# Attention softmax on eight cores: every second normalization on ScalarE, one merged copy out of PSUM

## The reference

```python
qkv = x @ Wqkv + bqkv
q, k, v = jnp.split(qkv, [D, D + KV], axis=-1)      # 16 heads of q, 4 of k and v, HD = 128
scores = jnp.einsum('bqhd,bkhd->bhqk', q, k) / HD
prob = jax.nn.softmax(scores, axis=-1)
out = jnp.einsum('bhqk,bkhd->bqhd', prob, v).reshape(b, s, D)
return out @ Wout + bout
# the layer: xn = layernorm(x); x + attention(xn) + experts(xn)
```

## Time and profile before

| | |
|---|---|
| median of 3 runs | 5502.65 us (lowest 5501.75) |
| the profiled execution | 5507.19 us, its span 5505.6 |
| spans of the cores | 5484.4 to 5505.6 us, core 6 the slowest |
| busy | PE 4952.2 (90%), DVE 1740.7 (32%), ACT 747.1 (14%), POOL 258.4 (5%) |
| chain that ended last | PE 86%, ACT 5%, DVE 4%, DMA 3%, issue 2% |
| attention | from 543 to 1134 us of the span |
| granted clock of the slowest core | mean 0.954 |

### The profile page before, as it was taken

The page is one execution under the profiler, slowest core; times in us unless marked ns, Lnnn a source line. Parts: engine busy times, 40 slices in busy tenths (PEclk is TensorE's granted clock), DMA queues, the critical chain, the costliest instruction groups (busy, mean ns, idle before and its releaser), DMA issues.

```text
span 5505.6 us, 63487 instructions; the slowest of 8 cores (5484.4 to 5505.6 us)
## 1 busy us (share of the span) xinstructions
PE 4952.2 (90%) x23551; PEld 2343.6 (43%) x24008; DVE 1740.7 (32%) x2608; ACT 747.1 (14%) x1045; POOL 258.4 (5%) x493
## 2 busy tenths in 40 slices
PE   3588666688999999999999999999999999999995
PEld 2434443343444444444444444444444444444443
DVE  3300666611232222323333322323223222333333
ACT  4311555521000000000000000000000000000000
POOL 0000000000000000000000000000000000000000
PEclk8589999999999999999999999999999999999997
DMA  5231000036444444444334444444444444434434
GB/s 171 77 63 30 1 1 1 1 58 104 73 73 74 75 74 73 74 74 75 70 70 78 73 73 77 74 75 75 73 73 73 74 75 74 73 69 71 79 54 122
DMA packets 79881, 378.32 MB, mean 69 GB/s; under 512 B 9696, under 2 KB 10848, under 8 KB 65248
## 3 DMA queue, kind: packets, MB, share of 16 engines
q0 software_dynamic: 70416, 323.03, 33.4%
q1 hardware_dynamic: 9168, 51.21, 2.9%
HBM read 688.80 MB, written 8.39 MB: 127 GB/s over the span
## 4 chain that ended last, share of the span: by engine, by line
PE 86%; ACT 5%; DVE 4%; DMA 3%; issue 2%; DVEq 0%; ACTq 0%; SPq 0%; POOLq 0%
PE ps_a L824 48%; PE ps_d L760 24%; PE ps_a L491 4%; ACT p_exp L578 3%; PE ps_a L682 2%; PE ps_a L563 2%; PE ps_c L792 1%; DMA x_re<-x_own 1%; PE ps_c L632 1%; PE ps_c L395 1%; PE ps_d L632 1%; DVE pnT L618 1%; DVE pn_sb L589 1%; DMA wgubuf<-gu 1%; PE ps_b L354 1%
## 5 line engine op out<-in xcount | busy, mean ns | idle before, releaser
L824 PE MATMUL ps_a<-xn_own,wgubuf 128*128 128x512 bf16 x12044 | 2692.1, 384 | 25.8 <-DMA wgubuf<-gu 11.9
L824 PEld LDWEIGHTS ps_a<-xn_own,wgubuf 128*128 128x128 bf16 x12288 | 1211.6, 99 | 1517.1 <-issue 103.3
L760 PE MATMUL ps_d<-hstash,wdbuf 128*128 128x512 bf16 x6016 | 1330.4, 379 | 10.8 <-DVE ffn_acc L770 0.4
L847 DVE TENSOR_TENSOR sg_sb<-ps_a,sg_sb 128x512 f32<-128x512 f32 x384 | 265.5, 691 | 2404.2 <-PE ps_a L824 2404.2
L760 PEld LDWEIGHTS ps_d<-hstash,wdbuf 128*128 128x128 bf16 x6144 | 595.9, 97 | 741.3 <-issue 182.0
L770 DVE TENSOR_TENSOR ffn_acc<-ffn_acc,ps_d 128x512 f32<-128x512 f32 x1024 | 704.3, 688 | 605.6 <-PE ps_d L760 602.2
L837 ACT ACTIVATE sg_sb<-ps_a 128x512 f32<-128x512 f32 x384 | 229.2, 597 | 2261.1 <-PE ps_a L824 2261.1
L60 POOL DMA_DIRECT2D wgubuf<-gu x384 | 202.6, 528 | 2604.0 <-PE ps_a L824 2555.1
L563 PE MATMUL ps_a<-k_sb,q_sb 128*128 128x512 bf16 x470 | 136.1, 412 | 204.5 <-ACT p_exp L578 132.0
L852 DVE TENSOR_TENSOR hstash<-sg_sb,c_rep 128x512 bf16<-128x512 f32 x384 | 266.0, 693 | 42.7 <-DVE sg_sb L847 3.6
L802 ACT ACTIVATE c_rep<-ps_c 128x512 f32<-128x512 f32 x64 | 38.2, 597 | 1534.5 <-PE ps_c L792 1534.5
(11 more groups left out here) (104 smaller groups left out, 1408.2 us busy)
## 6 DMA issues: line engine op xcount, KB each, us to landing
wgubuf<-gu POOLq DMA_DIRECT2D x384, 512.0 KB, 5.2
wdbuf<-down POOLq DMA_DIRECT2D x64, 1536.0 KB, 10.9
xtile<-x_own SPq DMA_DIRECT2D x16, 1024.0 KB, 5.7
xtile<-x_nbr SPq DMA_DIRECT2D x16, 1024.0 KB, 5.5
wjbuf<-wqkv POOLq DMA_DIRECT2D x24, 512.0 KB, 5.1
woutbuf<-wout POOLq DMA_DIRECT2D x16, 512.0 KB, 5.2
x_re<-x_own SPq DMA_DIRECT2D x8, 1024.0 KB, 8.5
o<-out_sb SPq DMA_DIRECT2D x8, 1024.0 KB, 6.0
```

Of the source, the lines that this page charges most:

```text
L760: ins = e_.matmul(ps_d[:, slot * 512:(slot + 1) * 512], wdbuf[gh % 3][:, (dc % 8) * 768 + icc * 128: (dc % 8) * 768 + icc * 128 + 128], hs ...
L824: ins = e_.matmul(ps_a[:, bank * 512:(bank + 1) * 512], wgubuf[bufi][:, dc * 128:(dc + 1) * 128], xn_own[:, dc * TOWN + tb * 512: dc * TOW ...
L847: ev_h1[(e, ip, tb)] = B.op("vector", lambda e_, tb=tb: e_.tensor_tensor(sg_sb[:, tb * 512:(tb + 1) * 512], ps_a[:, (2 + tb) * 512:(3 + tb ...
```

## The change

In attention, the norm of odd i moves to ScalarE, as an Identity activation with the reciprocal as its scale; it is emitted at the end of `emit_softmax(i)`, after the wait for the reciprocal and, where there is one, for the transposes of i-2 that read the same pn buffer. Even i keeps it on VectorE. ps_b becomes 2,048 bf16 elements wide (two banks); the 16 transposes of one i fill it, and one VectorE copy of 2,048 replaces the two of 1,024. TensorE waits once, for the copy of the i before, ahead of all 16. ps_c is now a view of the second bank of ps_b, and PV writes the two halves of ps_d.

```diff
@@ -245,10 +245,9 @@
     nc.bump_sbuf(MBASE + 204800 - nc.sbuf_base)
 
     ps_a = nc.alloc_psum_tensor("ps_a", [128, 2048], F32).ap()
-    ps_b = nc.alloc_psum_tensor("ps_b", [128, 1024], BF16).ap()
-    ps_c = nc.alloc_psum_tensor("ps_c", [128, 512], F32).ap()
+    ps_b = nc.alloc_psum_tensor("ps_b", [128, 2048], BF16).ap()
     ps_d = nc.alloc_psum_tensor("ps_d", [128, 1024], F32).ap()
-    ps_b2 = ps_d[:, 512:1024].bitcast(BF16)
+    ps_c = ps_b[:, 1024:2048].bitcast(F32)
 
     B = Builder(nc)
 
@@ -360,7 +359,7 @@
             B.wait("vector", "st", ev_tpb[t][k])
             dst_view = xn_dst.rearrange("p (c q) -> p c q", c=DC)[
                 :, 8 * k:8 * k + 8, (t % 8) * 128:(t % 8) * 128 + 128]
-            src_view = ps_b.rearrange("p (c q) -> p c q", c=8)
+            src_view = ps_b[:, 0:1024].rearrange("p (c q) -> p c q", c=8)
             ev_tpb_evac[t][k] = B.op("vector", lambda e, d=dst_view, s=src_view:
                                      e.tensor_copy(d, s), "sv")
 
@@ -537,7 +536,7 @@
                 B.wait("vector", "st", evt)
                 dstv = vt_sb[:, (g * 16 + 8 * k) * 128:(g * 16 + 8 * k) * 128 + 1024]
                 ev_vt_evac_last = B.op("vector", lambda e, d=dstv:
-                                       e.tensor_copy(d, ps_b[:]), "sv")
+                                       e.tensor_copy(d, ps_b[:, 0:1024]), "sv")
 
     B.barrier()
 
@@ -571,7 +570,7 @@
         qb2 = i % 2
         B.wait("scalar", "st", ev_sc)
         if i >= 2:
-            B.wait("scalar", "sv", ev_normC[i - 2])
+            B.wait("scalar", ev_normC[i - 2][0], ev_normC[i - 2][1])
             B.wait("scalar", "sv", ev_biasC[i - 2])
         else:
             B.wait("scalar", "sv", ev_nz)
@@ -583,47 +582,52 @@
         B.wait("vector", "ss", ev_ln)
         ev_biasC[i] = B.op("vector", lambda e, qb2=qb2: e.tensor_tensor(
             nmax2[qb2][:], nmax2[qb2][:], lns2[qb2][:], ALU.subtract), "sv")
-        B.op("vector", lambda e, qb2=qb2: e.reciprocal(rssum[:], ssum2[qb2][:]))
-        if (i - 2, 1) in ev_tpC:
-            B.wait("vector", ev_tpC[(i - 2, 1)][0], ev_tpC[(i - 2, 1)][1])
-        ev_normC[i] = B.op("vector", lambda e, qb2=qb2: e.tensor_scalar_mul(
-            pn_sb[qb2][:], p_exp[qb2][:], rssum[:]), "sv")
+        ev_rc = B.op("vector", lambda e, qb2=qb2: e.reciprocal(rssum[:], ssum2[qb2][:]), "sv")
+        if i % 2 == 0:
+            if (i - 2, 1) in ev_tpC:
+                B.wait("vector", ev_tpC[(i - 2, 1)][0], ev_tpC[(i - 2, 1)][1])
+            ev_normC[i] = ("sv", B.op("vector", lambda e, qb2=qb2: e.tensor_scalar_mul(
+                pn_sb[qb2][:], p_exp[qb2][:], rssum[:]), "sv"))
+        else:
+            B.wait("scalar", "sv", ev_rc)
+            if (i - 2, 1) in ev_tpC:
+                B.wait("scalar", ev_tpC[(i - 2, 1)][0], ev_tpC[(i - 2, 1)][1])
+            ev_normC[i] = ("ss", B.op("scalar", lambda e, qb2=qb2: e.activation(
+                pn_sb[qb2][:], p_exp[qb2][:], AF.Identity, scale=rssum[:]), "ss"))
 
     def emit_tp(i):
         h, q = divmod(i, 8)
         qb2 = i % 2
-        B.wait("tensor", "sv", ev_normC[i])
+        B.wait("tensor", ev_normC[i][0], ev_normC[i][1])
+        if psb_gen[0] is not None:
+            B.wait("tensor", psb_gen[0][0], psb_gen[0][1])
         for k in range(2):
-            pbank = ps_b if k == 0 else ps_b2
-            if psb_gen[k] is not None:
-                B.wait("tensor", psb_gen[k][0], psb_gen[k][1])
-
-            def pt_batch(e, k=k, qb2=qb2, pbank=pbank):
+            def pt_batch(e, k=k, qb2=qb2):
                 for j in range(8):
                     kc = 8 * k + j
-                    ins = e.matmul(pbank[:, j * 128:(j + 1) * 128],
+                    ins = e.matmul(ps_b[:, k * 1024 + j * 128: k * 1024 + (j + 1) * 128],
                                    pn_sb[qb2][:, kc * 128:(kc + 1) * 128],
                                    ident_b[:], is_transpose=True,
                                    start=(j == 0), stop=(j == 7))
                 return ins
             ev_pt = B.op("tensor", pt_batch, "st")
             ev_tpC[(i, k)] = ("st", ev_pt)
-            dst_view = pnT.rearrange("p (c q2) -> p c q2", c=DC)[
-                :, 8 * k:8 * k + 8, q * 128:q * 128 + 128]
-            src_view = pbank.rearrange("p (c q2) -> p c q2", c=8)
-            B.wait("vector", "st", ev_pt)
-            if h >= 1 and q == 0:
-                B.wait("vector", "st", ev_pvmm.get((h - 1, 1)))
-            evc = B.op("vector", lambda e, d=dst_view, s=src_view:
-                       e.tensor_copy(d, s), "sv")
-            psb_gen[k] = ("sv", evc)
+        dst_view = pnT.rearrange("p (c q2) -> p c q2", c=DC)[
+            :, :, q * 128:q * 128 + 128]
+        src_view = ps_b.rearrange("p (c q2) -> p c q2", c=DC)
+        B.wait("vector", "st", ev_tpC[(i, 1)][1])
+        if h >= 1 and q == 0:
+            B.wait("vector", "st", ev_pvmm.get((h - 1, 1)))
+        evc = B.op("vector", lambda e, d=dst_view, s=src_view:
+                   e.tensor_copy(d, s), "sv")
+        psb_gen[0] = ("sv", evc)
 
     def emit_pv(h):
         g = h % G
         B.wait("tensor", psb_gen[0][0], psb_gen[0][1])
         B.wait("tensor", "sv", ev_pv_vlast[0])
         for qb in range(2):
-            pv_ps = ps_c if qb == 0 else ps_d[:, 0:512]
+            pv_ps = ps_d[:, 0:512] if qb == 0 else ps_d[:, 512:1024]
             if h >= 1:
                 B.wait("tensor", "ss", ev_pvout[(h - 1, qb)])
 
```

## The result

The time of the changed kernel stands to that of the kernel before as 1.023, 95% interval 1.0213 to 1.0246, so it is slower: 5623.8 to 5634.65 us against 5499.25 to 5507.19. The profiled execution took 5634.65 us, its span 5633.1 on core 0 (before: 5507.19 and 5505.6 on core 6), so 127.5 us more.

What follows compares the result with a forecast made beforehand. The prediction took attention to be bound by the chain exp, scores, exp at 3.49 us. It summed 85 us for the norm's place and 34 for the clock, about 120 us more, giving 5622 us, range 5582 to 5675.

Steps and rivals of the forecast that it cites:

- part 6 of the sum: Attention: longer TensorE idle lowers its clock in nearly every pair, and it recovers; 34 us net.
- The bound: Attention: the chain exp, scores, exp holds an iteration at 3.49 us, so freeing nearly full VectorE can't shorten it.
- The norm's place: ScalarE's order: the odd norm delays the next exp, 5.27 instead of 3.49 us; 48 x 1.78 = 85 us.
- The cover of the PV: Fifteen odd norms just ahead of a PV end under it and cost nothing; uncovered they would cost 27 us.
- The merged copy: VectorE's copy of 2048, taken as 1.29 us: hidden at full clock, costs 0.45 us at low clock.
- a sign of error: Attention: a step over a PV longer than 12 us would show the cover of the PV wrong.
- rival B: Attention: low clock nearly throughout, 159 us more, 5662, or 5679 if it reaches the PV's first third; chance 0.16.
- A: Attention: the clock stays as it was or recovers before it hurts; 85 us more, 5588; chance 0.22.
- C: Attention: VectorE sets the period, so not slower; gain at most 30.7 us, 5472; chance 0.03.
- D: ScalarE reloads its function table for each odd norm and back; 126 us more, 5748; chance 0.02.
- The chances: Whole kernel: slower by over 2% (110 us, 5612.7) 0.52, within 2% 0.46, faster by over 2% 0.02.

Runs made afterwards that it cites:

- the fills: Useless matmuls in TensorE's idle: ten per even block without PV on the changed kernel, 5580.3 and 5581.2 us; six per PV iteration on merge only, 5495.3 to 5498.4 us.
- merge only: Changed kernel with all norms kept on VectorE, so only the merged copy and the new places of ps_c and PV's sums: 5499.6 us.
- PV spread: Merge only with a head's 32 PV matmuls in 8 pieces, one an iteration, and PV evacuations behind an exp: 5375.4 and 5372.7 us.
- the cut chain: PV spread with scores and exp in halves, bf16 p_exp, later Ln, half sums added on VectorE: 5330.6 to 5381.7 us, ratio to before 0.9713.

## What held of the prediction, and the step that failed

The forecast was 5622 us and slower; the runs lie at 5624 to 5635, inside 5582 to 5675. The step that failed is the clock term, part 6 of the sum: it was put at 34 us net and measured 40 by the fills, 44.6 by the steps. By its steps:

- **The bound.** Chain exp, scores, exp at 3.49 beside a nearly full VectorE: shown by merge only, which takes work off VectorE and gains nothing. PV spread and the cut chain, which gain 127 and some 165 us with every norm on VectorE, agree with it, though the latter changes VectorE's work too.
- **The norm's place, 85 us.** Measured 48 x 1.76 = 84.5, and 87 to 89 with the steps that the fill left at low clock. The step was forecast at 5.27 and is 5.25; the norm at 1.99 us and is 2.002. For an ACTIVATE with one pointer operand the Trainium skill (ScalarE: Activation LUTs, What ACT_TABLE_LOAD costs) gives 186 ns, 0.833 ns an element and 93 for the pointer; for 2048 elements that makes 1985 ns as an estimate, and the trace agrees within 1%.
- **The cover of the PV.** 15 odd norms cost nothing at full clock: with fill the PV step is 10.97, as before.
- **The merged copy.** Taken as 1.29, it is 1.224. Nothing at full clock, and at low clock the odd step was forecast at 5.72 and is 5.68.
- **The clock, 34 us: the step that failed.** Its mechanism was right: low clock behind the long idle, and back again within the head. Its size was not. The sum charged 0.55 of the price of a stage at low clock throughout, a share for which no row stood. Before what the kernel before pays is taken off, that is 29 us for the even steps (0.55 x 0.83 x 64), 12 for the odd ones (0.55 x 0.45 x 48) and 7 for the scores ahead of the PV (0.55 x 0.83 x 15), 48 in all; the changed kernel's steps lie above 3.49, 5.25 and 10.97 by 34, 13 and 13 us, 60 in all. The share of the even steps is 0.64, and it isn't spread evenly over the pairs, as the sum had it: the even step directly behind a PV never pays and most others pay in full, so that 0.55 came near is luck.
- **The PV steps within that term.** They cost twice what was put down, since I had counted only the scores ahead of the products: where TensorE enters the PV at low clock, the first products run slow too (six in 2.76 us). They went from 11.03 to 11.81 on average, with single ones of 13.38, past the 12 us that the prediction had named as a sign of error; the sum had left this to rival B. Before pays 13.5 us in the sum and 15.6 by its steps. The Trainium skill (TensorE: Matmul & The Clock Gate, HAM oscillation — how this bites in real kernels) describes a kernel whose short bursts between waits start at low clock each time; most scores behind an idle of 3.3 us do so here.
- **The rivals.** A (85 us) would have needed the clock of the kernel with fill. C fell with merge only. D fell with the page: three table loads in the span, as before.
- **The chances.** 0.52 for slower by over 2% against 0.46 for within: 127 us lies 17 above the bound of 110, and 6 to 10 of those 17 are the mis-sized clock.

## What to carry to other kernels

Before moving work to an idle engine, look where in that engine's order it will stand and which chain passes that point: an instruction of 2.0 us in front of the next exp cost 1.76, though ScalarE was idle 86% of the span, and relieving a fuller engine beside the chain gained nothing. A longer iteration also left TensorE idle for longer, and what its clock then lost came on top (40 of 129 us); a fill of useless matmuls measures that part nearly by itself. The idle to look for is the wait that an order creates without need: spreading the PV over eight iterations, with its evacuations behind an exp, gave 127 us with the same matmuls, exps and norms.

## What the runs showed of the hardware

- TensorE ran four scores at low clock (1.86 instead of 1.02 us) after idles of 3.3 us in most pairs of the changed kernel, attention's granted clock 0.78, but not in the pair directly behind a PV (652.48: 1.02 after 2.15 idle). Ten useless matmuls of 0.23 us in the idle of 3.3 us brought the clock to 0.97, and the program to 50 us less.
- With the same work for TensorE the granted clock of attention was 0.98 with PV spread and 0.83 with PV spread and the odd norm on ScalarE; even steps at low clock cost that kernel 47 us.
- In the kernel with the norm behind the next exp ScalarE began an exp 0.20 us after its own norm (norm ends 706.36, exp 706.56); in the changed kernel it does so after 0.10 (714.22 and 714.32). Why they differ isn't known.
